# Second router: the low part of one expert weight made by GpSimd instead of VectorE

## The reference

```python
x = x + tanh(g_xattn[0]) * _L0_xattn_ref(ctx, ctx, _layernorm(x), ...)
x = x + tanh(g_ffn[0])   * _L0_ffn_ref(_layernorm(x), ...)
x = x + tanh(g_xattn[1]) * _L1_xattn_ref(_layernorm(x), ctx, ctx, ...)
x = x + tanh(g_ffn[1])   * _L1_ffn_ref(_layernorm(x), Wg, W1, W2)

def _L1_ffn_ref(x, Wg, W1, W2):          # TOP_K = 2, 8 experts, hidden 256
    logits = einsum('btd,de->bte', x, Wg)
    probs = softmax(logits)
    top_w, top_i = top_k(probs, 2)       # normalised to a sum of 1, made dense: combine
    h = square(relu(einsum('td,edh->teh', xt, W1)))
    y = einsum('teh,ehd->ted', h, W2)
    out = einsum('te,ted->td', combine, y)
```

## Time and profile before

| | |
|---|---|
| median of three runs | 2166.19 us |
| profiled execution, its own time | 2167.3 us |
| its span | 2165.3 us |
| mean granted clock of TensorE | 0.971 |
| second router's block | 1770.5 to 1803.7 us of the span |

### The profile page before, as it was taken

One profiled execution on the slowest core, in us unless ns is written; L12 is line 12 of the kernel. 1 busy time (PEld: TensorE's weight loads), 2 busy tenths in 40 slices (PEclk: granted clock), 3 DMA queues, 4 the chain that ended last, 5 costly groups with the idle time before them and its releaser, 6 DMA issues. The chain is left out here.

```text
span 2165.3 us, 82956 instructions
## 1 busy us (share of the span) xinstructions
PE 2034.1 (94%) x28380; PEld 1569.5 (72%) x28380; DVE 1895.2 (88%) x4324; ACT 1579.7 (73%) x3515; POOL 1573.0 (73%) x1456
## 2 busy tenths in 40 slices
PE   3999999977999999999999799999999957999999
PEld 2788888854666666666666699999999944666666
DVE  6899999986888888888888689999999968888888
ACT  3788888875555555555655678888888856888887
POOL 1577777642666666666666799999999933888887
PEclk9999999987999999999999899999999978999999
DMA  5000000002322222222220355555555520000000
GB/s 179 16 7 6 7 6 6 7 2 65 110 86 86 78 82 88 78 82 89 79 78 30 63 83 89 84 89 86 89 87 87 82 59 1 15 10 15 10 15 15
DMA packets 476587, 121.41 MB, mean 56 GB/s; under 512 B 431895, under 2 KB 446871, under 8 KB 475876
## 3 DMA queue, kind: packets, MB, share of 16 engines
q1 hardware_dynamic: 476228, 120.41, 24.8%
q10 hardware_dynamic: 288, 0.07, 0.0%
HBM read 106.51 MB, written 13.89 MB: 56 GB/s over the span
## 5 line engine op out<-in xcount | busy, mean ns | idle before, releaser
L1286 POOL TENSOR_TENSOR f_low<-f_hidden,f_high 128x512 f16<-128x512 f32 x336 | 442.6, 1323 | 217.1 <-ACT f_high L1218 215.3
L1244 DVE TENSOR_TENSOR f_hidden<-f_hidden,f_share 128x512 f32<-128x512 f32 x336 | 372.4, 1109 | 0.0
L1433 POOL TENSOR_TENSOR f_low<-f_hidden,f_high 128x512 f16<-128x512 f32 x256 | 297.0, 1161 | 74.6 <-ACT f_high L1376 74.0
L1224 ACT ACTIVATE f_act_out<-f_gate 128x512 f32<-128x512 f32 x336 | 200.5, 597 | 192.6 <-PE f_gate L1188 192.5
L1267 DVE SCALAR_TENSOR_TENSOR f_hidden<-f_up,f_act_out 128x512 f32<-128x512 f32 x336 | 229.6, 684 | 83.6 <-PE f_up L1188 52.1
L1218 ACT ACTIVATE f_high<-f_hidden 128x512 f16<-128x512 f32 x336 | 210.4, 626 | 72.8 <-DVE f_hidden L1244 71.5
L1198 PE MATMUL f_y<-w_high,f_high 128*128 128x128 f16 x1344 | 242.5, 219 | 2.2 <-POOL f_low L1286 2.2
L1198 PE MATMUL f_y<-w_low,f_high 128*128 128x128 f16 x1344 | 242.4, 219 | 0.0
L1198 PE MATMUL f_y<-w_high,f_low 128*128 128x128 f16 x1344 | 242.4, 219 | 0.0
L1810 POOL TENSOR_TENSOR a_q_head_high<-a_q_t_high,a_head_mask 128x2048 f16<-128x2048 f16 x64 | 232.9, 3640 | 7.2 <-DVE a_q_t_low L1860 3.2
L1810 POOL TENSOR_TENSOR a_q_head_low<-a_q_t_low,a_head_mask 128x2048 f16<-128x2048 f16 x64 | 233.0, 3640 | 0.0
(11 more groups left out here) (279 smaller groups left out, 8173.7 us busy)
## 6 DMA issues: line engine op xcount, KB each, us to landing
f_share<-expert_shares SPq DMA_DIRECT2D x128, 256.0 KB, 3.2
a_q_pos<-queries SPq DMA_DIRECT2D x64, 512.0 KB
f_share<-expert_shares SPq DMA_DIRECT2D x128, 128.0 KB, 2.9
relative_values<-a_rel_all SPq DMA_DIRECT2D x512, 8.0 KB
f_share<-expert_shares SPq DMA_DIRECT2D x128, 32.0 KB, 1.8
queries<-a_q_parts SPq DMA_DIRECT2D x64, 64.0 KB, 3.2
a_rel<-relative_values SPq DMA_DIRECT2D x64, 64.0 KB, 2.1
out_x<-x_all SPq DMA_DIRECT2D x16, 256.0 KB, 2.0
```

Of the source, the lines that this page charges most:

```text
L1224: nc.scalar.activation(act_out[m % RING][:, :], gate_ps[m % BANKS][:, :], ACT.Silu, scale=1.0 / WSCALE).then_inc(act_ready, 1)
L1244: nc.vector.tensor_tensor(hidden[r][:, :], hidden[r][:, :], share[k][:, :, :].rearrange("p t q -> p (t q)"), ALU.mult).then_inc(scaled, 1)
L1286: nc.gpsimd.tensor_tensor(low[r][:, :], hidden[r][:, :], high[r][:, :], ALU.subtract).then_inc(low_ready, 1)
L1433: nc.gpsimd.tensor_tensor(low[k][:, :], hidden[k][:, :], high[k][:, :], ALU.subtract).then_inc(low_ready, 1)
```

## The change

GpSimd gets two more jobs for the second weight (`split[1]`): it multiplies a group of it by WSCALE in place, and later makes its low part as t32 - high. VectorE keeps the low part of the first weight only. ACT's cast of the second weight waits for GpSimd's scaling (`weights_scaled`) and has the factor 1. GpSimd's order becomes, for g from 0 to 23: normalize(g), scale_weights(g - 2), low_weights(g - 8), each where its group exists.

```diff
+        weights_scaled, weights_high = sem("weights_scaled"), sem("weights_high")
@@ GpSimd
-                for g in range(G):
+                def scale_weights(g):
+                    if weights and inside(g, 0, G):
+                        pool.wait_ge(stage_in[1], 16 * len(stage_cuts[1]))
+                        t32 = split[1][0]
+                        nc.gpsimd.tensor_scalar(t32[:, g, :], t32[:, g, :], WSCALE, None,
+                                                ALU.mult).then_inc(weights_scaled, 1)
+
+                def low_weights(g):
+                    if weights and inside(g, 0, G):
+                        pool.wait_ge(weights_high, g + 1)
+                        t32, high, low = split[1]
+                        nc.gpsimd.tensor_tensor(low[:, g, :], t32[:, g, :], high[:, g, :], ALU.subtract)
+
+                for g in range(G + 2 * stack):
                     normalize(g)
+                    scale_weights(g - 2)
+                    low_weights(g - 2 * stack)
@@ VectorE, low_weights
-                        for t32, high, low in split:
+                        for t32, high, low in split[:1]:
@@ ACT, high_weights
-                        for arrived, cuts, (t32, high, _) in zip(stage_in, stage_cuts, split):
-                            act.wait_ge(arrived, 16 * len(cuts))
-                            last = nc.scalar.activation(high[:, g, :], t32[:, g, :], ACT.Copy, scale=WSCALE)
+                        act.wait_ge(stage_in[0], 16 * len(stage_cuts[0]))
+                        act.wait_ge(weights_scaled, g + 1)
+                        for (t32, high, _), scale in zip(split, (WSCALE, 1.0)):
+                            last = nc.scalar.activation(high[:, g, :], t32[:, g, :], ACT.Copy, scale=scale)
                         last.then_inc(weights_high, 1)
```

More of the change, by code:

```diff
@@ L758, in stacked_router @@
         stage_in = [sem(f"stage{k}_in") for k in range(len(weights))]
-        weights_high = sem("weights_high")
+        weights_scaled, weights_high = sem("weights_scaled"), sem("weights_high")
         def by_pool(g):
```

## The result

The changed kernel took 2174.09 us (median of 7 runs, 2172.27 to 2175.78), the kernel before 2169.47 in the runs that stand beside them (7 runs). The ratio is 1.0022, 95% interval 1.0013 to 1.0032: slower, by 4.6 us between the medians (4.8 by the ratio), and within the 0.3% that the prediction called no change. The profiled execution has a span of 2170.2 us against 2165.3. Three executions of the later experiments, of 7052, 8074 and 8756 us, stand far apart from all others and are in no ratio.

What follows compares the result with a forecast made beforehand. VectorE led the router stage before; after the change GpSimd would be slowest, waiting for the second weight. Queue +1.9 us and PE's clock 0.7 made +2.6, giving a median of 2168.8 us, range 2164.2 to 2173.2.

Steps and rivals of the forecast that it cites:

- Direction and mechanism: Router stage: GpSimd's scaling waits 4.6 us for the second weight, delaying VectorE's normalisation 7 by 1.7 us; slower, chance 0.68.
- the second rival: First scaling: weights land early enough or the wait counts less, VectorE keeps its saving; up to 1.6 us faster, chance 0.08.
- the replay: Router stage: engine queues stepped through in order with assumed pitches, before and after; the difference gave +1.9 us, +2.6 with clock.
- the sum of GpSimd's queue behind the landing: GpSimd after the second weight lands: 24.65 us of work plus 2.4 us of waits, ending at 1804.8.
- The first case: GpSimd's wait and queue, with a scaling of 0.3 to 0.6 us: +1.3 to +4.3 us, 2168.8 us, chance 0.68.
- The scaling: GpSimd's in-place multiplication of 128x128 f32 by a constant, taken at 0.42 us, nearest to a TENSOR_TENSOR row of 427 ns.
- The low clock: PE pauses from 1774.2 to 1779.0, so its clock stays low up to 1783: 0.7 us later.
- Contention: GpSimd and VectorE slow each other: 0.7 us within the range, or +7.1 us by a shared-port rule, chance 0.06.
- the strong rule: Two-input VectorE instructions and GpSimd SBUF reads share one port: 4.5 us on GpSimd's queue, 2173.3 us, chance 0.06.
- VectorE 1.57 us for a group: VectorE's round per group of four images, 1.77 us before less 0.20 for one moved subtraction.
- no standstill: Two VectorE weight subtractions beside a GpSimd normalisation took 0.61 us against 0.48 alone: 0.13 us more, without blocking.
- The dear scaling (0.85 us): Rival: GpSimd's constant scaling costs as its two-operand form, so GpSimd alone bounds the stage: +6.5 us, 2172.7, chance 0.18.

Runs made afterwards that it cites:

- the other time: The changed kernel run once more, unaltered: block 37.08 us against 37.60 the first time; ratio of totals to the kernel before 1.0015.
- the run with tensor_tensor: Against the change, GpSimd's scaling written as tensor_tensor with a broadcast constant: block 36.87 us against 37.60; ratio to the kernel before 1.0012.
- the run with PE kept busy: Against the change, 22 extra PE transposes of the identity between the turns of groups 2 and 3: block 36.39 us against 37.60; ratio to before 1.0017.
- the short copy: Against the change, GpSimd's subtraction replaced by a tensor_copy reading one tensor: block 36.60 us against 37.60; one execution.
- the long one-input instruction: Against the change, GpSimd's subtraction replaced by a tensor_scalar times 1.0: block 36.91 us, 37.92 to the next stage, as in the change; one execution.
- the run with the low part alone: Against the change, no scaling of the second weight; GpSimd only makes its low part: block 31.31 us against before's 32.87; ratio to before 0.9979.

## Why the prediction was right or wrong, point by point

- **Direction and mechanism: right.** GpSimd came to the wait after 3 normalisations, stood 4.69 us (said: 4.6), and VectorE's normalisation 7 moved. Moving the scaling alone removes all of the loss. Loading earlier gives it back one for one, as the second rival had it. But that rival put the break-even at a landing at 1775.6, 5.1 us into the block. In the run with the second weight first it landed 4.8 us into it, and the block was still 2.4 us longer than before: by the replay it should have been 0.3 shorter, so the replay is 2.7 us too low there and 2.1 for the change.
- **Size: +2.6 said, +4.7 in the block (+4.2 the other time).** This is the step that failed: the sum of GpSimd's queue behind the landing. It had 24.65 us of work and 2.4 us of waits for casts, 3.1 with the clock's 0.7; the trace has 29.84 us from 1778.22 to 1808.06, of which 3.95 are waits (0.6, 0.7 and 1.1 said; 1.74, 0.90 and 1.31 measured) and 25.9 work. The first case's own bounds, +1.3 to +4.3, did not hold the change. The terms behind it that were mis-sized:
  - *The scaling*, taken at 0.42, was 0.53 us. By the run with tensor_tensor 0.136 us is worth 0.73 at most, so 0.11 is worth up to 0.6. The range held it; the choice did not. The other way to write the same arithmetic, which I took as nearest, measured 0.40. The operation's name was the better guide than its arithmetic.
  - *The low clock*, taken at 0.7 (low up to 1783), lasted until about 1786, and came back later in the block (0.50 from 1793.6 to 1799.2, as before from 1788.8 to 1795.2), where the replay had none. By the run with PE kept busy the early part is 1.2: 0.5 more.
  - *Contention*, taken at nothing in the sum, with 0.7 from the rows and 4.5 by the strong rule as a rival: 1.0 at most, by the short copy, and some 0.3 if the copy's being shorter is taken off at the rate of the scaling. I had looked at the wrong pair. I priced VectorE's weight subtractions beside GpSimd; it was VectorE's normalisations that stretched, by 0.18 us for three. The subtractions do collide too: three of GpSimd's 16, the ones that start with VectorE's, took 0.53 us, the others 0.42, and VectorE's go up to 0.51.
  - Together 2.6 + 0.6 + 0.5 + (0.3 to 1.0) = 4.0 to 4.7. The terms are from separate runs, each good to some 0.5 us, so their shares are not settled: the traces show the longer scalings, the late clock and the longer normalisations, but what each of them costs is an estimate.
- **"VectorE 1.57 us for a group": wrong.** It was 1.75 in the change; with the long one-input instruction on GpSimd, where nothing slows the normalisations, it was 1.57 (1795.73 to 1797.30). GpSimd's own round, said to be the slowest at 1.70, was 1.76. That 3.2 us taken off VectorE became 1.6 in the run with the low part alone has this reason in part (0.9 us); 0.7 us are longer waits for the casts.
- **The rule on contention.** The Trainium skill (SBUF — State Buffer, Who interferes with whom) says that VectorE's tensor_scalar can run in a mode that takes both ports, and then GpSimd and it block each other. The trace agrees that normalisations suffer and not only instructions with two inputs. The page makes no difference by the number of tensors that GpSimd reads; here there was one: 0.85 us beside one tensor read, 1.03 beside two. For the weight subtractions the strong rule would have put 4.5 us on GpSimd's queue, and in the change it did not: 13 of its 16 subtractions took 0.42 us, the 428 ns of the earlier trace rows. But that is partly a matter of time, since most of them start when VectorE's is about to end. Where the two meet, GpSimd is held by more than the prediction's "no standstill" allows: subtractions of 0.51 us with tensor_tensor, a scaling of up to 0.72 instead of 0.53 with the long one-input instruction, and a normalisation of 1.19 instead of 0.80 beside two subtractions, which is nearly the 0.40 that the two take.
- **The dear scaling (0.85 us)** was not it. The total of +4.6 us lies between that rival's 6.5 and the forecast's 2.6, but the instruction was 0.53 us and the rest came by other terms.
- **The absolute time.** 2174.1 is above the range's 2173.2. The kernel before measured 2166.2 in the three runs shown and 2169.5 in seven: 3.3 us of the 5.3 between 2174.1 and the forecast's 2168.8 are the yardstick, 2.0 are the forecast.

## What to carry to other kernels

Before work is given to an engine with idle time, lay the new instruction's waits beside the clock time at which the engine gets there: an engine that runs ahead of the others has slack because of what stands in its queue, and one wait for a load spends it for all that follow. Place the first such instruction at the landing (here behind the sixth or seventh normalisation instead of the third). And do not count work moved from VectorE to GpSimd at its full saving where the new instruction reads two tensors. Here 3.2 us were moved and 1.6 arrived, since VectorE's other instructions became longer and the casts were not ready earlier. Last, see which engine ends a block after the move: with the wait gone it was GpSimd.

## What was not expected of the hardware

- GpSimd's tensor_scalar with one constant takes 532 ns for 128x128 f32, the same product as tensor_tensor with a broadcast operand 396 ns, a cast 0.28 us.
- Three VectorE tensor_scalars with per-partition operands take 0.85 to 0.88 us beside a GpSimd cast (0.28 us) or scaling by a constant (0.53 us), and 1.03 beside a subtraction of two tensors (0.42 us). Beside a normalisation of GpSimd that starts with them they once took 1.00.
- A GpSimd normalisation of 0.80 us took 1.19 beside two VectorE subtractions of two tensors each.
- A pause of 5 us on PE right where its clock had risen before kept it at 0.50 for 11 us more; with PE kept busy through the pause it rose at the old place.
